# Field moments by tile: z sums and a perceptron for each tile of 128 samples, in place of one for two tiles

## The reference

```python
e = stack([tbl_f[ids[:, f]] for f in range(26)], axis=1)     # 512 x 26 x 32
x1 = einsum('bik,bjk,hij->bhk', e, e, W1) + b1               # h: 128
x2 = einsum('bik,bjk,hij->bhk', x1, e, W2) + b2
z = sum(concatenate([x1, x2], axis=1), axis=-1)              # 512 x 256
h = concatenate([z, dense_ctx], axis=1)                      # 512 x 272
h = maximum(h @ W_top1 + b_top1, 0)                          # 512 wide
h = maximum(h @ W_top2 + b_top2, 0)                          # 256 wide
y = h @ W_top3                                               # 512 x 1
```

## Time and profile before

| what | value |
|---|---|
| median of 3 runs | 196.22 us |
| the profiled execution | 195.79 us |
| its span | 194.0 us |
| its mean granted clock | 0.886 |
| PE busy | 142.2 us |
| DVE busy | 97.1 us |
| ACT busy | 89.7 us |
| POOL busy | 109.2 us, to slice 30 of 40 |

### The profile page before, as it was taken

One profiled execution on the slowest core, in us unless ns is written; L12 is line 12 of the kernel. 1 busy time (PEld: TensorE's weight loads), 2 busy tenths in 40 slices (PEclk: granted clock), 3 DMA queues, 4 the chain that ended last, 5 costly groups with the idle time before them and its releaser, 6 DMA issues.

```text
span 194.0 us, 2531 instructions
## 1 busy us (share of the span) xinstructions
PE 142.2 (73%) x861; PEld 117.2 (60%) x861; DVE 97.1 (50%) x305; ACT 89.7 (46%) x298; POOL 109.2 (56%) x110
## 2 busy tenths in 40 slices
PE   0099999909995900599999705994089699799994
PEld 0095343309994600599988505994068399788882
DVE  6856399199831598255863520367962036400010
ACT  0257999974895485324100395234623733200111
POOL 3777788788877777777777777777840000000000
PEclk9999999995896975589999985699559999999999
DMA  5880010010001110001110101101100000000000
GB/s 148 335 209 12 12 17 7 11 14 14 7 12 32 21 15 14 10 15 17 31 19 11 14 14 17 14 14 15 32 14 0 0 0 3 4 20 0 0 5 0
DMA packets 8107, 5.57 MB, mean 29 GB/s; under 512 B 4477, under 2 KB 7565, under 8 KB 7966
## 3 DMA queue, kind: packets, MB, share of 16 engines
q0 software_dynamic: 3328, 1.71, 6.0%
q1 hardware_dynamic: 2862, 3.31, 5.3%
q10 hardware_dynamic: 1904, 0.38, 1.2%
HBM read 4.93 MB, written 0.00 MB: 25 GB/s over the span
## 4 chain that ended last, share of the span: by engine, by line
POOL 42%; PE 31%; issue 17%; DVE 5%; DMA 3%; ACT 1%; DVEq 0%
POOL rows L228 42%; PE p_t L593 9%; PE p_z L614 7%; PE p_t L601 5%; DVE region L447 3%; PE p_h L643 2%; PE p_w L643 2%; PE p_z L655 2%; PE p_x L655 2%; DMA idx<-in_ids 1%; DMA rows<-in_tbl,idx 1%; PE p_x L665 1%; DVE eT L436 1%; ACT region L295 1%; PE p_x L614 1%
## 5 line engine op out<-in xcount | busy, mean ns | idle before, releaser
L228 POOL DMA_INDIRECT rows<-in_tbl,idx x104 | 108.5, 1043 | 33.5 <-issue 31.4
L593 PE MATMUL p_t<-e_diag,pairs 128*124 128x108 f32 x128 | 21.0, 319 | 13.1 <-issue 8.5
L614 PE MATMUL p_z<-region 124*128 124x256 f32 x128 | 28.0, 380 | 1.0 <-ACT region L268 1.0
L593 PE MATMUL p_t<-region 128*124 128x108 f32 x128 | 18.4, 291 | 12.9 <-ACT region L258 11.8
L266 ACT COPY region<-p_t 124x352 f32<-124x352 f32 x32 | 14.4, 450 | 29.2 <-PE p_t L593 29.2
L593 PEld LDWEIGHTS p_t<-e_diag,pairs 128*124 128x124 f32 x128 | 19.0, 229 | 14.3 <-issue 14.3
L543 DVE COPY L<-p_t 74x208 f32<-74x208 f32 x24 | 8.9, 371 | 36.7 <-PE p_t L601 36.7
L614 PEld LDWEIGHTS p_z<-region 124*128 124x128 f32 x128 | 24.2, 190 | 4.4 <-ACT region L268 1.1
L593 PEld LDWEIGHTS p_t<-region 128*124 128x124 f32 x128 | 16.5, 203 | 13.5 <-issue 13.5
L436 DVE STREAM_TRANSPOSE eT<-rows 128x160 f32<-128x160 f32 (+2 forms) x20 | 9.8, 492 | 16.4 <-DMA rows<-in_tbl,idx 16.4
L447 DVE TENSOR_TENSOR pairs<-eT 128x32 f32<-128x32 f32 (+13 forms) x52 | 16.9, 393 | 0.3
(11 more groups left out here) (90 smaller groups left out, 195.9 us busy)
## 6 DMA issues: line engine op xcount, KB each, us to landing
region<-in_L_rec_W SPq DMA_DIRECT2D x1, 1664.0 KB, 8.4
rows<-in_tbl,idx POOLq DMA_INDIRECT x104, 2.4
wt<-in_W_top SPq DMA_DIRECT2D x2, 512.0 KB
w<-in_L_rec_W ACTq DMA_DIRECT2D x1, 338.0 KB, 5.9
gmix<-L SPq DMA_DIRECT2D x4, 56.0 KB
gmix<-L SPq DMA_DIRECT2D x4, 30.0 KB
gmix<-L SPq DMA_DIRECT2D x4, 28.0 KB
idx<-in_ids SPq DMA_DIRECT2D x1, 52.0 KB, 2.5
```

What stands on the lines that cost most here:

```text
L228: pool.indirect_dma_start(rows[:, t, f * EMB:(f + 1) * EMB], None, tables[f], bass.IndirectOffsetOnAxis(ap=idx[:, t, f:f + 1], axis=0),).t ...
L593: last = nc.tensor.matmul(p_t[0][k % 2][0:ROWS0, b * w:(b + 1) * w].rearrange("p (q j) -> p q j", q=QUADS), pairs[t % 2][:, s, 0:ROWS0], e ...
L614: last = nc.tensor.matmul(out, w, x, start=(n == 0), stop=(n == len(terms) - 1))
```

## The change

Each tile gets z sums and a perceptron of its own, at 128 columns: all of `z`, `h1`, `h2` and the PSUM sums are 128 wide, and `z_sums` and its followers run four times. `T` has two buffers, taken by turns (`t % 2`), of the same size together. `gmix` is one tile wide, so its DMAs wait until the z sums of the tile before are done. On PE the order becomes, for each tile: dense part; a wait until two groups of the next tile are multiplied (`HELD = 2`; not in the last tile); z sums; perceptron; moments of the next tile. ACT runs `save_z` and `save_h1` of the tile before behind the spread of group 1, and `save_h2` and `save_y` behind that of group 2. DVE's order stays as it was.

```diff
-DUO = 2
-N = DUO * P
-DUOS = TILES // DUO
-HELD = 3
+HELD = 2
...
-        T = region3[:, :].rearrange("p (s n) -> p s n", n=N)
+        T = region3[:, :].rearrange("p (i s n) -> p i s n", i=2, n=P)
-        gmix = sb("gmix", [P, 2, N])
+        gmix = sb("gmix", [P, 2, P])
...
                 sp.wait_ge(t_saved[1], TURNS * (t + 1))
-                half = slice(t % DUO * P, (t % DUO + 1) * P)
+                if t:
+                    sp.wait_ge(z1_done, t)
...
             for t in range(1, TILES):
-                for g in range(NG):
-                    if t == TILES - 1 and g == HELD:
-                        save_h1(0)
-                        save_h2(0)
-                        save_y(0)
-                    spread(t, g)
+                spread(t, 0)
+                spread(t, 1)
+                save_z(t - 1)
+                save_h1(t - 1)
+                spread(t, 2)
+                save_h2(t - 1)
+                save_y(t - 1)
+                spread(t, 3)
+                spread(t, 4)
                 for k in range(TURNS):
                     save_first(t, k)
-                if t % DUO:
-                    save_z(t // DUO)
+            save_z(LAST)
             save_h1(LAST)
...
             def z_sums(t):
                 for chunk in (0, 1):
-                    pe.wait_ge(t_saved[chunk], TURNS * DUO * (t + 1))
+                    pe.wait_ge(t_saved[chunk], TURNS * (t + 1))
...
-            turns(1)
-            dense_part(0)
-            z_sums(0)
-            turns(2)
-            pe.wait_ge(pairs_ready, NG * (TILES - 1) + HELD)
-            h1_sums(0)
-            h2_sums(0)
-            y_sums(0)
-            dense_part(1)
-            turns(3)
-            z_sums(1)
-            h1_sums(1)
-            h2_sums(1)
-            y_sums(1)
+            for t in range(TILES):
+                dense_part(t)
+                if t < LAST:
+                    pe.wait_ge(pairs_ready, NG * (t + 1) + HELD)
+                z_sums(t)
+                h1_sums(t)
+                h2_sums(t)
+                y_sums(t)
+                if t < LAST:
+                    turns(t + 1)
```

More of the change, by code:

```diff
@@ L171, in program @@
         MOVES = 3
-        LAST = DUOS - 1
+        LAST = TILES - 1
         def f_count(j):
@@ L179, in h1_sum, with columns @@
             bank = (p_h1, p_w)[c // 2]
-            return bank[:, c % 2 * N:(c % 2 + 1) * N]
+            return bank[:, c % 2 * P:(c % 2 + 1) * P]
         def h2_sum(c):
[L183 to L188, removed]
+            return p_x[:, P:2 * P] if c == 0 else p_z2[:, P:2 * P]
+        def columns(k):
+            return slice(k * TURN * QUADS, (k + 1) * TURN * QUADS)
         block = ctx.enter_context(nc.Block())
@@ L205, in _ @@
                 sp.wait_ge(t_saved[1], TURNS * (t + 1))
-                half = slice(t % DUO * P, (t % DUO + 1) * P)
+                if t:
+                    sp.wait_ge(z1_done, t)
                 for part, (c0, c1) in enumerate(MIX):
-                    sp.dma_start(gmix[0:(c1 - c0) * A, part, half],
+                    sp.dma_start(gmix[0:(c1 - c0) * A, part, :],
                                  L[MID:ROWS1, c0 - A:c1 - A, :]).then_inc(mix_in[t], 16)
-                sp.dma_start(gmix[MIX_ROWS[1] - MID:MIX_ROWS[1], 1, half], L[0:MID, NB, :]).then_inc(mix_in[t], 16)
-            sp.wait_ge(y_saved, DUOS)
+                sp.dma_start(gmix[MIX_ROWS[1] - MID:MIX_ROWS[1], 1, :], L[0:MID, NB, :]).then_inc(mix_in[t], 16)
+            sp.wait_ge(y_saved, TILES)
             sp.dma_start(y.rearrange("b o -> o b"), yrow[:, :, :, :].rearrange("o t q s -> o (t q s)")
@@ L353, in save_second @@
                 bank = p_t[1][k % 2]
-                cols, here = columns(t, k), slice(k * TURN * QUADS, (k + 1) * TURN * QUADS)
+                cols = columns(k)
                 sums = bank[:, 0:TURN * SINGLES1 * QUADS].rearrange("p (b q s) -> p s b q", b=TURN, q=QUADS)
-                engine_copy(L[0:ROWS1, :, here].rearrange("p s (b q) -> p s b q", q=QUADS),
+                engine_copy(L[0:ROWS1, :, cols].rearrange("p s (b q) -> p s b q", q=QUADS),
                             sums[0:ROWS1, A - CUT:SINGLES1, :, :])
-                engine_copy(T[0:HALF, SINGLES0:SLOTS, cols].rearrange("p s (b q) -> p s b q", q=QUADS),
+                engine_copy(T[0:HALF, t % 2, SINGLES0:SLOTS, cols].rearrange("p s (b q) -> p s b q", q=QUADS),
                             sums[0:HALF, 0:NEW, :, :])
-                return engine_copy(T[HALF:P, LONG:SLOTS, cols].rearrange("p s (b q) -> p s b q", q=QUADS),
+                return engine_copy(T[HALF:P, t % 2, LONG:SLOTS, cols].rearrange("p s (b q) -> p s b q", q=QUADS),
                                    sums[0:HALF, NEW:NEW + UPPER, :, :])
@@ L558, in _ @@
             dve.wait_ge(h2_done, LAST)
-            dve.wait_ge(h1_done, 2 * DUOS)
+            dve.wait_ge(h1_done, 2 * TILES)
             for c in (2, 3):
@@ L630, in z_sums @@
                     pe.wait_ge(z_saved, 2 * t)
-                weighted(p_z2[:, 0:N], [(WT[0:ROWS0, s, :], T[0:ROWS0, s, :]) for s in range(SLOTS) if s != Z1_ONE]
+                weighted(p_z2[:, 0:P], [(WT[0:ROWS0, s, :], T[0:ROWS0, t % 2, s, :]) for s in range(SLOTS) if s != Z1_ONE]
                          ).then_inc(z2_done, 1)
-                for i in range(DUO):
-                    pe.wait_ge(mix_in[DUO * t + i], 16 * MOVES)
-                weighted(p_x[:, 0:N], [(WT[0:ROWS0, Z1_ONE, :], T[0:ROWS0, Z1_ONE, :])]
+                pe.wait_ge(mix_in[t], 16 * MOVES)
+                weighted(p_x[:, 0:P], [(WT[0:ROWS0, Z1_ONE, :], T[0:ROWS0, t % 2, Z1_ONE, :])]
                          + [(WT[0:MIX_ROWS[m], Z1_MIX + m, :], gmix[0:MIX_ROWS[m], m, :]) for m in (0, 1)]
@@ L664, in y_sums @@
                         pe.wait_ge(h2_saved, t + 1)
-                    last = nc.tensor.matmul(p_x[0:1, 0:N], wt3[:, k:k + 1], h2[:, k, :],
+                    last = nc.tensor.matmul(p_x[0:1, 0:P], wt3[:, k:k + 1], h2[:, k, :],
                                             start=(k == 0), stop=(k == TOP2 // P - 1))
```

33 lines of the change are left out of this document (16 added, 17 removed).

## The result

The changed kernel takes **202.18 us** (median of 4 runs, 201.59 to 203.07) against 196.59 us for the one before (4 runs): a ratio of **1.030**, 95% interval 1.022 to 1.038. Forecast were 202.4 us and "slower". The profiled execution took 201.78 us, with a span of 200.0.

A forecast was written before the change was run, and what follows sets the result against it. It saw a gather-paced front of 146 us and a PE-bound tail. Three 39.4 us rounds from 67.4 reach 185.6; 0.1, 8.1 and 6.8 make the span 200.6, plus 1.8 is 202.4 us (8 in 10: 196.5 to 206.0).

The forecast's parts named there:

- this closes a loop through PE, DVE and ScalarE, which it runs three times: Z sums wait for DVE's second group of the next tile, taken after this tile's moments are saved: 39.4 us a round.
- groups 0 and 1, start of PE: PE stands before the z sums while DVE multiplies the next tile's first two groups: 5.85 us plus 0.05 start.
- z sums behind a pause: 70 records on PE, 22 at half clock (0.226 us) and 48 at full (0.116): 10.6 us.
- a record of 128 columns: In PE's z sums, 0.116 us at full clock, near the lower of the bounds 0.112 and 0.220.
- from the z sums to the moments: Perceptron on PE and ScalarE, with group 2's spread in the way and groups 3 and 4's last: 8.5 us.
- moments, to DVE's next group (the last: to the z sums): PE's moments until DVE has saved them, at half clock at first after a 4.7 us pause: 14.4 us.
- perceptron and store at the end: Behind tile 3's z sums, relus shared with DVE, then the store to the end of the span: 6.8 us.
- the first rival: The clock holds in the pause before the moments: three rounds lose 5.4 us, giving 197.0 us; chance 10%.
- the clock holds in both pauses: Full clock before z sums too, so they take 8.1 us: another 7.5 us off, 189.5 us; chance 8%.
- Narrow matmuls as dear as wide ones: Weight loads keep a z-sum record at up to 0.220 us: 224.7 us in the worst case; chance 5%.
- the loop is not closed: A counted wait is met earlier; with gathers still pacing the front, tile 3's moments start at 146.7, total 176.0; chance 3%.
- The gathers were to all but vanish from the chain: Sign on the changed kernel's chain: the loop starts behind DVE's weight copies, not behind a gather.

The follow-up runs named there:

- no_hold: The changed kernel without PE's held wait before the z sums: 281.5 us, 0.947 in the slow first batch; run again (_b), 178.6 us, 0.915.
- spreads_first_b: The changed kernel with all five spreads on ScalarE ahead of the copies of z, held wait kept, second run: 184.8 us, 0.943.
- filled_b: The changed kernel with idle PE filled by matmuls whose results are unused, held wait kept, second run: 189.9 us, 0.965.
- wide_spreads_first: The kernel before (256 columns) with ScalarE's copies of z of tiles 0 and 1 behind all spreads of tile 2: 192.3 us, 0.984.
- no_hold_warm: The changed kernel without the held wait, with unused matmuls added behind the y matmuls to keep the clock: 178.9 us, 0.914 of the medians.
- held1_b: The changed kernel with z sums waiting for one group of the next tile, not two, second run: 189.2 us, 0.961.
- held4: The changed kernel with z sums waiting for four groups of the next tile, not two: 212.8 us, 1.083.

## Why the prediction was right

The sign and the size came out by the mechanism that was forecast. That the span was met to 0.6 us owes something to luck: the z sums were forecast 1.0 us too long in three rounds together, the moments 0.7 and the tail 0.4 too short.

**The loop.** The step "this closes a loop through PE, DVE and ScalarE, which it runs three times" decided the sign. It was forecast at 39.4 us a round; DVE's first groups start at 67.23, 106.17 and 145.85, and tile 3's z sums at 184.90: 38.9, 39.7 and 39.1. no_hold shows that the loop is closed by the wait: one wait removed, 22.7 us gone.

**The terms**, forecast and measured in the changed kernel:

| term | forecast | measured |
|---|---|---|
| groups 0 and 1, start of PE | 5.9 | 5.9 |
| z sums behind a pause | 10.6 | 10.5, 9.8, 10.5 |
| z sums, full clock | 8.1 | 7.9 |
| a record of 128 columns | 0.116 | 0.115 |
| from the z sums to the moments | 8.5 | 8.4, 8.5, 8.5 |
| moments, to DVE's next group (the last: to the z sums) | 14.4 | 14.2, 15.5, 14.2 |
| perceptron and store at the end | 6.8 | 7.2 |
| start of tile 3's moments | 171.2 | 170.7 |
| span | 200.6 | 200.0 |

Two of the prediction's sums are slightly off: 22 records at 0.226 and 48 at 0.116 make 10.5, not 10.6, and by its own numbers the perceptron and store at the end lose 3.9 us (10.7 to 6.8), not some 3.7. Neither changes a verdict; the measured loss is 3.5.

The term with the widest bounds, a record at 128 columns (0.112 to 0.220), came out beside the row that it was nearest to. The slope that the Trainium skill gives in TensorE: Matmul & The Clock Gate, "Back-to-back issue gap", would have made it 0.18, an estimate from the page's 81 and 131 ns; the trace does not agree: 0.115 against 0.220 at 256 columns, 0.52 of it. Four narrow z sums cost PE 4 x 7.9 = 31.7 us at the full clock, two wide ones 2 x 15.2 = 30.4, so the split itself was nearly free.

**The smallest error that could have grown** is the clock before the moments. I expected it to be lost, as it was, but took one length for all restarts. The measured moments differ by 1.3 us between rounds, and before those of tiles 1 and 3 the clock fell only as PE came back. spreads_first_b, which takes this pause away, shows what the first rival priced: moments of 12.6 us.

**The rivals.** That the clock holds in both pauses was priced at 189.5 us. filled_b is this case made by force: 189.9, of which 2.0 are the fillers' own delay. Narrow matmuls as dear as wide ones: refuted by the 7.38 us row. That the loop is not closed was priced at 176.0 with the gathers still in front: no_hold_b, which opens it, takes 178.6. Its moments of tile 3 start at 146.41, forecast 146.7, but by ScalarE and not by the gathers, which were 0.4 us ahead. That sum also forgot the half clock in tile 3's moments (14.2 in place of 12.6).

**A pointer that was off.** The gathers were to all but vanish from the chain. They have 13% of it: those of tile 0, up to 36.2 us, still hold the moments of tile 0, ahead of the loop. I had looked at the loop's start alone.

## What to carry to other kernels

Before a stage is cut into smaller pieces, write down the round that each piece will make through the engines, with every wait and every copy ahead of it in program order, and compare it with the pace of what feeds it: here 39 us a round against 34 between the last gathers of tiles 2 and 3 (fields there at 111.3 and 145.25). A wait that holds an engine back so that something else can go first is worth a try without it, and a copy belongs where its engine is idle, unless what it waits for comes later than what stands behind it. A narrower stage gives back in the tail what its width took, and loses what the longer round puts in front of its last piece: tile 3's moments started at 155.5 before, at 170.7 in the change, at 155.0 in spreads_first_b and at 146.4 in no_hold_b.

## What the runs showed of the hardware

- **The length of a short pause does not tell whether the granted clock is kept.** It was kept over 0.57 us (filled_b), 1.15 (before) and 2.70 (wide_spreads_first, 1.00 all through the moments behind it), and lost around pauses of 1.97 (no_hold_warm), 2.35 (before), 2.97 and 3.05 us (the change, held1_b). At one and the same place of the program, ahead of the matmuls that transpose the worked-out weights, PE stood 2.59 us in the change and 2.58 in no_hold_warm: in the first the clock fell 1.3 us after PE came back (four records took 1.11 us at 61.44), in the second it stayed whole (0.65 us at 61.45).
- **It can also fall while PE works.** In no_hold_b it was 1.00 in the pause of 2.98 us and until 147.4, one microsecond into tile 3's moments, and 0.53 in the 3.1 us behind. Behind a fall the half clock lasted from 3.4 to 5.9 us of work in the changed kernel.
- **A float32 matmul with 128 columns of weights and 128 moving columns takes 0.230 us in a stream** (two records of 0.115), and 0.44 us with 256 moving columns. So here half the moving columns took 0.52 of the time.
- **In one batch of runs a stage of small hand-overs was 100 us slower, and nothing else was.** There, PE worked out `F` with 3.5 us of idle time before each matmul:

```profile
94.35 2.04 PE L582 MATMUL p_t<-S,region 128*128 128x509 f32 x2 [3.62 <-issue]
99.87 2.06 PE L582 MATMUL p_t<-S,region 128*128 128x509 f32 x2 [3.48 <-issue]
```

  while rounds later in the same trace were 30.5 and 30.6 us. Most of the time lies between PE and ScalarE: the matmul of 94.35 ends at 96.39, and ScalarE's copy of its sums starts only at 99.23 (0.58 us long), after which PE starts within 0.1 us. The profile puts ScalarE's waits down to a source that it does not show. Nor is it shown to be the chip: the record gives the first batch the same chip number as held4, held1_b, filled_b and spreads_first_b, which ran that stage as the change did. The cause stays open; no run was made for it. Ratios within that batch compare like with like, but the extra time shrinks them: held1 and filled were 1.6% and 1.7% faster than the kernel before there, and 3.9% and 3.5% in the later batch. The 22.7 us of the held wait are 11% of 202.2, and would be 7.5% of the 304 (281.5 + 22.7) that the change would take there.
